# Query projection in three float32r passes, rope in one set, output weights' low part on GpSimd

## What is computed

```python
x = x + xattn(layernorm(x), ctx, ctx)          # sigmoid attention over the context, one head
h = layernorm(x)
c_kv = h @ W_kv_down                           # 512 -> 128
k_rope = rotary(c_kv @ W_k_rope);  k = c_kv @ W_k_up;  v = c_kv @ W_v_up
q = h @ W_q;  q_rope = rotary(h @ W_q_rope)    # 16 heads of 32, rope of 32 shared by the heads
scores = (q·k + q_rope·k_rope) / 8, causal, softmax
x = x + (softmax @ v) @ W_o
x = x + ffn(layernorm(x))                      # 8 experts, top 1, relu(g)^2 * u
```

## Time and profile before

| | us |
|---|---|
| median of 3 runs | 578.97 (578.73 to 578.99) |
| profiled execution | 580.1 |
| its span, first to last instruction | 578.3 |
| PE busy | 570.2 |
| DVE busy | 454.7 |
| ACT busy | 399.6 |
| POOL busy | 1.7 |

### The profile page before, as it was taken

One profiled execution on the slowest core, in us unless ns is written; L12 is line 12 of the kernel. 1 busy time (PEld: TensorE's weight loads), 2 busy tenths in 40 slices (PEclk: granted clock), 3 DMA queues, 4 the chain that ended last, 5 costly groups with the idle time before them and its releaser, 6 DMA issues.

```text
span 578.3 us, 7988 instructions
## 1 busy us (share of the span) xinstructions
PE 570.2 (99%) x2986; PEld 477.8 (83%) x2986; DVE 454.7 (79%) x507; ACT 399.6 (69%) x536; POOL 1.7 (0%) x7
## 2 busy tenths in 40 slices
PE   7999999999999999999999999999999999999998
PEld 4788888888888888888888888888888887867887
DVE  5887878787878898889787978887878787888742
ACT  5876766767677877778777777776767665587321
POOL 1000000000000000000000000000000000000000
PEclk8999999999999999999999999999999999999999
DMA  8567777777778877777778878767676745000201
GB/s 322 189 221 233 246 223 250 225 222 237 218 221 252 240 261 239 243 253 255 224 252 251 254 222 256 231 206 225 212 224 213 227 143 212 1 2 2 73 1 37
DMA packets 33238, 115.89 MB, mean 200 GB/s; under 512 B 4080, under 2 KB 4784, under 8 KB 32944
## 3 DMA queue, kind: packets, MB, share of 16 engines
q1 hardware_dynamic: 32768, 115.05, 62.9%
q10 hardware_dynamic: 432, 0.33, 0.2%
HBM read 114.84 MB, written 0.52 MB: 199 GB/s over the span
## 4 chain that ended last, share of the span: by engine, by line
PE 94%; ACT 2%; DVE 2%; DMA 1%; issue 0%; ACTq 0%
PE ps L384 45%; PE ps L328 23%; PE ps L346 12%; PE ps L876 4%; PE ps L908 2%; PE ps L557 2%; PE ps L764 1%; PE ps L491 1%; ACT w L693 1%; PE ps L671 1%; DMA x_s<-in_x 1%; PE ps L700 1%; PE ps L282 0%; PE ps L467 0%; ACT zh L360 0%
## 5 line engine op out<-in xcount | busy, mean ns | idle before, releaser
L384 PE MATMUL ps<-nh,zh 128*128 128x512 f32 x392 | 144.3, 390 | 0.2 <-ACT zh L360 0.2
L384 PE MATMUL ps<-nh,zl 128*128 128x512 f32 x392 | 144.2, 389 | 0.1
L384 PE MATMUL ps<-nl,zh 128*128 128x512 f32 x392 | 144.1, 389 | 0.0
L361 DVE TENSOR_TENSOR zl<-zf,zh 128x1024 fp32r<-128x1024 f32 x49 | 60.1, 1226 | 82.9 <-ACT zh L360 82.9
L247 DVE TENSOR_TENSOR nl<-rawn,nh 128x1024 fp32r<-128x1024 f32 x97 | 115.4, 1220 | 2.2 <-issue 0.8
L233 DVE TENSOR_TENSOR tl<-rawt,th 128x1024 fp32r<-128x1024 f32 x96 | 112.8, 1216 | 0.0
L244 ACT ACTIVATE nh<-rawn 128x1024 fp32r<-128x1024 f32 x97 | 100.7, 1056 | 13.5 <-DMA rawn<-in_ctxn 12.8
L356 ACT ACTIVATE zf<-ps 128x512 f32<-128x512 f32 x98 | 58.4, 597 | 56.9 <-PE ps L346 51.0
L228 ACT ACTIVATE th<-rawt 128x1024 fp32r<-128x1024 f32 x96 | 96.4, 1052 | 0.9 <-DMA rawt<-in_ctxt 0.8
L384 PEld LDWEIGHTS ps<-nh,zh 128*128 128x128 f32 x392 | 73.4, 188 | 15.9 <-ACT zh L360 0.6
L384 PEld LDWEIGHTS ps<-nh,zl 128*128 128x128 f32 x392 | 73.5, 188 | 15.7 <-DVE zl L361 0.5
(11 more groups left out here) (182 smaller groups left out, 605.0 us busy)
## 6 DMA issues: line engine op xcount, KB each, us to landing
rawn<-in_ctxn SPq DMA_DIRECT2D x97, 512.0 KB, 6.5
rawt<-in_ctxt SPq DMA_DIRECT2D x96, 512.0 KB, 5.0
h_s<-in_wg SPq DMA_DIRECT2D x4, 512.0 KB, 6.7
h_s<-in_wu SPq DMA_DIRECT2D x4, 512.0 KB, 6.9
wds<-in_wd SPq DMA_DIRECT2D x4, 512.0 KB, 5.7
raw<-in_ctxt SPq DMA_DIRECT2D x2, 512.0 KB, 8.3
h_s<-in_wvt SPq DMA_DIRECT2D x2, 512.0 KB, 7.9
wq_s<-in_wq SPq DMA_DIRECT2D x1, 1024.0 KB, 5.0
```

The costliest lines, as they stand in the source:

```text
L361: ZL[b] = put("vector", lambda e: e.tensor_tensor(zl[b % 2][:], zf[:], zh[b % 2][:], ALU.subtract), [ZH[b]] + av, "zl")
L384: AV[b] = put("tensor", lambda e, z=z, n=n, i=i, j=j, r=r: e.matmul(bank(4 + r), z[:, j * T + r * P:j * T + r * P + P], n[:, j * D:(j + 1) ...
```

## The change

It gives the query projection the three-pass form: `wq` is split into `wqh` (ACT) and `wql` (DVE, in place of `wq_s`), `hT` into `hqh` and `hql`. It makes the rope of queries and keys of one row half as one set (both products in one bank, three DVE instructions of 32x256, spreads of 32x2048 on DVE alone), reorders the k copies, moves the subtractions for `wol` from DVE to GpSimd and behind query tile 3, and the first two loads of `wd` behind it too, because `wqh` lies where `wds` is.

```diff
+        wql = once("wql", [P, 4, D], F32R)
...
+        wqh = once("wqh", [P, 4, D], F32R)
         wds = [sb(f"wds{i}", [P, 1024]) for i in range(2)]
         wdh = sb("wdh", [P, 8, D], F32R)
+        hqh, hql = several("hq", 2, [P, 4, T], F32R)
...
-        qa = sa("qa", [P, 8, T])
-        ka = sa("ka", [P, 8, T])
+        qk = sa("qk", [P, 16, T])
+        qa, ka = qk[:, 0:8], qk[:, 8:16]
...
-                    DWD = [dma("sync", wds[k][:], wd[:, 2 * k:2 * k + 2, :].rearrange("p a b -> p (a b)"), f"dwd{k}",
-                               [KP[NB - 1]]) for k in range(2)]
...
         def split_o(k):
...
-            return lambda: put("vector", lambda e: e.tensor_tensor(flat(wol[:, n]), flat(wo_s[:, n]), flat(woh[:, n]),
-                                                                   ALU.subtract), [hi], "wol")
+            return lambda wait: put("gpsimd", lambda e: e.tensor_tensor(flat(wol[:, n]), flat(wo_s[:, n]), flat(woh[:, n]),
+                                                                        ALU.subtract), [hi, *wait], "wol")
+        def split_q(k):
+            n = slice(2 * k, 2 * k + 2)
+            WQH.append(put("scalar", lambda e: e.activation(flat(wqh[:, n]), flat(wq_s[:, n]), ACT.Copy), [DWQ2, KP[last]],
+                           "wqh"))
+            return lambda: WQL.append(put("vector", lambda e: e.tensor_tensor(
+                flat(wql[:, n]), flat(wq_s[:, n]), flat(wqh[:, n]), ALU.subtract), [WQH[k]], "wql"))
+        def split_h(r):
+            n = half(r)
+            HQH.append(put("scalar", lambda e: e.activation(hqh[:, :, n], hT[:, :, n], ACT.Copy), HT[r], "hqh"))
+            return lambda: HQL.append(put("vector", lambda e: e.tensor_tensor(
+                hql[:, :, n], hT[:, :, n], hqh[:, :, n], ALU.subtract), [HQH[r]], "hql"))
...
         table(ACT.Sqrt)
+        low_q = [split_q(0)]
         YA = sum_out(0)
...
         XM = [project_v(0, 2, [ZF[last]])]
+        low_q.append(split_q(1))
         low_o = [split_o(k) for k in range(2)]
...
-        low_o[0]()
+        low_q[0]()
...
-        WOL = low_o[1]()
+        low_q[1]()
+        split_h(0)()
         XM.append(project_v(1, 3, []))
...
-            KR[r] = put("tensor", lambda e: e.matmul(bank(b_c)[:, 0:P], kr_s[:], ckv[:, n], start=True, stop=True),
+            KR[r] = put("tensor", lambda e: e.matmul(bank(b_q)[:, P:T], kr_s[:], ckv[:, n], start=True, stop=True),
...
+        def rope(r, bk):
+            n = half(r)
+            for k in range(2):
+                a = bank(bk)[32 * k:32 * k + 32, 0:T].rearrange("p (w n) -> p w n", w=2)
+                c = cs_s[32 * k:32 * k + 32, n].rearrange("p (o n) -> p o n", o=1).to_broadcast([32, 2, P])
+                m = put("vector", lambda e, k=k, a=a, c=c: e.tensor_tensor(rt[:, k, :, n], a, c, ALU.mult), [KR[r]], "rt")
+            return lambda: put("vector", lambda e: e.tensor_tensor(rt[:, 2, :, n], rt[:, 0, :, n], rt[:, 1, :, n], ALU.add),
+                               [m], "rt")
+        def spread(r, u, mark):
+            n = half(r)
+            d = qk[64 * u + 32:64 * u + 64, :, n].rearrange("p (w s) n -> p w s n", w=2)
+            a = rt[:, 2, :, n].rearrange("p w (o n) -> p w o n", o=1).to_broadcast([32, 2, 8, P])
+            ROT.setdefault(r, []).append(put("vector", lambda e: e.tensor_copy(d, a), [mark], "ro"))
...
+        def query(ts, outs, wait):
+            steps = [(wqh, hqh, HQH + WQH), (wql, hqh, WQL), (wqh, hql, HQL)]
+            for i in range(3):
+                w, h, ready = steps[i]
+                for k, t in enumerate(ts):
+                    n = slice(P * t, P * t + P)
+                    for c in range(4):
+                        done = (i, k, c) == (2, len(ts) - 1, 3)
+                        m = put("tensor", lambda e, w=w, h=h, c=c, i=i, k=k, n=n, done=done: e.matmul(
+                            outs[k], w[:, c, n], h[:, c, :], start=(i == 0 and k == 0 and c == 0), stop=done),
+                            [*ready, *wait], "q" if done else None)
+            return m
...
         values_up(0, 6, 1)
+        add = rope(0, 2)
         HT.append([put("vector", lambda e: e.tensor_scalar(hT[:, 0:2, half(1)], chunks(0)[:, 0:2], 2.0, None, ALU.mult),
...
-        k_copies(0, 4, range(2, 4))
-        f = turned(0, 0, 2, QR[0])
-        spread(0, 0, qa, f, 0)
-        spread(0, 0, qa, f, 1)
+        f = add()
+        low_h = split_h(1)
         latents(1, 5, 7, 3, 0, [YB[1]])
         values_up(1, 0, 1)
+        low_h()
+        spread(0, 0, f)
+        spread(0, 1, f)
+        k_copies(0, 4, range(2, 4))
         VE[0] = put("scalar", lambda e: e.activation(v_s[:, 0, :], bank(6), ACT.Copy), [VT[0]], "ve_a")
         table(ACT.Exp)
-        f = KT0 = turned(1, 0, 1, KR[0])
-        spread(1, 0, ka, f, 0)
-        spread(1, 0, ka, f, 1)
-        k_copies(1, 3)
-        query(0, bank(1)[:, 0:T], [KT0, *HT[1], DWQ2])
-        QT = query(1, bank(1)[:, T:2 * T], [])
-        f = turned(0, 1, 7, QR[1])
-        spread(0, 1, qa, f, 0)
-        spread(0, 1, qa, f, 1)
-        f = turned(1, 1, 5, KR[1])
+        k_copies(1, 3, range(2))
+        QT = query([0, 1], [bank(1)[:, 0:T], bank(1)[:, T:2 * T]], [])
+        g = rope(1, 7)()
+        spread(1, 0, g)
         q_copies(0, QT, bank(1).rearrange("p (t n) -> p t n", t=2), lambda i: slice(i // 2, 4, 2))
-        spread(1, 1, ka, f, 0)
-        QT = query(2, bank(2)[:, 0:T], ROT[0, 0])
+        spread(1, 1, g)
+        QT = query([2], [bank(2)[:, 0:T]], [f])
+        k_copies(1, 3, range(2, 4))
         VE[1] = put("scalar", lambda e: e.activation(v_s[:, 1, :], bank(0), ACT.Copy), [VT[1]], "ve_a")
...
-                [*QA[0], *ROT[0, 0], *ROT[1, 0], KA[0], VE[0]]
+                [*QA[0], *ROT[0], KA[0], VE[0]]
...
         q_copies(1, QT, bank(2)[:, 0:T], lambda i: 4 + i // 2)
-        spread(1, 1, ka, f, 1)
-        QT = query(3, bank(1)[:, 0:T], QA[0])
+        QT = query([3], [bank(1)[:, 0:T]], QA[0])
+        for low in low_o:
+            WOL = low([QT])
+        DWD = [dma("sync", wds[k][:], wd[:, 2 * k:2 * k + 2, :].rearrange("p a b -> p (a b)"), f"dwd{k}", [QT])
+               for k in range(2)]
         exps(0)
```

More of the change, by code:

```diff
@@ L170, in program @@
         v_s = sa("v_s", [P, 2, D])
-        qa = sa("qa", [P, 8, T])
-        ka = sa("ka", [P, 8, T])
+        qk = sa("qk", [P, 16, T])
+        qa, ka = qk[:, 0:8], qk[:, 8:16]
         rtx = ExitStack()
-        rt = rtx.enter_context(nc.sbuf_tensor("rt", [32, 6, T], F32))
+        rt = rtx.enter_context(nc.sbuf_tensor("rt", [32, 3, 2, T], F32))
         rtx.close()
@@ L498, in split_o @@
             hi = put("scalar", lambda e: e.activation(flat(woh[:, n]), flat(wo_s[:, n]), ACT.Copy), [DWO], "woh")
-            return lambda: put("vector", lambda e: e.tensor_tensor(flat(wol[:, n]), flat(wo_s[:, n]), flat(woh[:, n]),
-                                                                   ALU.subtract), [hi], "wol")
+            return lambda wait: put("gpsimd", lambda e: e.tensor_tensor(flat(wol[:, n]), flat(wo_s[:, n]), flat(woh[:, n]),
+                                                                        ALU.subtract), [hi, *wait], "wol")
+        WQH, WQL, HQH, HQL = [], [], [], []
+        def split_q(k):
[9 more added lines that the diff above has]
+                hql[:, :, n], hT[:, :, n], hqh[:, :, n], ALU.subtract), [HQH[r]], "hql"))
         def col(r, k, n=1):
@@ L559, in project @@
             return m
-        CKV, QR, KR, KT, VT = ({} for _ in range(5))
+        CKV, KR, KT, VT = ({} for _ in range(4))
         def latents(r, b_c, b_q, b_k, b_v, wait):
@@ L566, in latents @@
             CKV[r] = put("scalar", lambda e: e.activation(ckv[:, n], bank(b_c)[:, 0:P], ACT.Copy), [m], "ckv")
-            QR[r] = project(bank(b_q)[:, 0:P], lambda c: qr_s[:, c, :], n, [X1[r], YT[1][0]], "qr")
-            KR[r] = put("tensor", lambda e: e.matmul(bank(b_c)[:, 0:P], kr_s[:], ckv[:, n], start=True, stop=True),
+            project(bank(b_q)[:, 0:P], lambda c: qr_s[:, c, :], n, [X1[r], YT[1][0]], "qr")
+            KR[r] = put("tensor", lambda e: e.matmul(bank(b_q)[:, P:T], kr_s[:], ckv[:, n], start=True, stop=True),
                         [CKV[r]], "kr")
@@ L613, in q_copies @@
             QA[g] = done
-        def query(t, o, wait):
-            return project(o, lambda c: wq_s[:, c, P * t:P * t + P], slice(0, T), wait, "q")
+        def query(ts, outs, wait):
[10 more added lines that the diff above has]
+            return m
         latents(0, 1, 2, 4, 6, [])
```

## The result

The changed kernel takes 579.94 us (median of 19 runs, 579.76 to 581.15) against 578.94 for the kernel before (19 runs): a ratio of 1.0017 with a 95% interval of 1.0011 to 1.0024. It is a microsecond **slower**, where a gain of 0.7 was forecast.

The account below looks back on a forecast made before the run. PE matmuls bound the stage up to the first scores, ACT sets the pace after 510.97. PE's 0.86 us saving, with 0.15 given back and copies rounding off, nets -0.69: median 578.3, range 577.3 to 581.0.

Parts of the forecast that it names:

- wol on GpSimd: Output weights' low-part subtractions queued on GpSimd after query tile 3, about 511.0; 2.2 us each, needed at 528.07, costing nothing.
- rival 1: GpSimd holds up DVE's small multiplication behind the second unit's maxima; 1.4 us reach the chain, 579.7; chance 0.33.
- The small step: DVE multiplication by a constant after the second unit's maxima, due at 513.61; held until GpSimd ends at 515.4.
- Cover 0.40: Slack of 0.40 us before the third unit's maxima, leaving 1.4 of the 1.8 us lateness on the chain.
- The three passes: Query tiles 0 and 1 on PE as three float32r passes: 2.88 us in place of 3.46; tile 2 1.44, from 1.73.
- the sum of -0.69: Forecast total: first scores start at about 507.83 in place of 508.52, all other parts adding nothing; median 578.3.
- the sign to look for, 8.4 us: If right, first scores come 8.4 us behind the second half's first latent product, 9.2 before.
- The 0.15 given back by DVE ahead of HT: Rope products and the rows' split delay DVE's half of HT; PE starts at about 499.45 instead of 499.30.
- Splitting wq: ACT copies of 1.05 us fit idle time, leaving 0.85 us cover before the first evacuation; DVE subtractions cost nothing.
- Rival 2: Doubled spreads on DVE run at one element a cycle, 2.28 us each, 1.06 more; 581.6; chance 0.07.
- Rival 3: More is won through hidden slack on DVE and ACT's lighter queue: 577.0 to 577.8, middle 577.4; chance 0.13.
- wd loads: Two wd loads moved behind the wait for query 3 on SP; data wanted 17 us later, so no cost.

## Why the prediction was wrong

The sign was wrong, and one step is to blame: **"wol on GpSimd ... Hidden in any case unless it holds up another engine"** was priced at nothing in the forecast, and rival 1, which gives it a price, got a chance of 0.33 against 0.40. It does hold up DVE: the step takes 2.18 us in place of 0.17, and 1.53 us of that reach the chain. Rival 1 said 579.7; 579.94 was measured. Its steps:

- GpSimd's work: 2.2 each assumed, 2.33 measured; from 511.30 (511.0 forecast).
- The small step is late by 1.8: 2.01 measured (2.18 - 0.17).
- Cover 0.40, so 1.4 on the chain: 1.5 measured.
- The sign to look for was given wrongly: "an idle time of DVE ahead of that small step". The step itself gets longer.

The evidence was at hand: the rows showed that this form of operation is faster out of SBUF than out of PSUM at 128x512, 0.55 against 0.68. That the step over two numbers runs in the same form was inferred from its opcode; its 0.17 us can't show a rate.

The Trainium skill (SBUF — State Buffer, "Who interferes with whom") says that a DVE instruction in a two-port mode and one of GpSimd exclude each other for the whole instruction, and that a DVE instruction with two SBUF inputs contends with a GpSimd one that reads SBUF. The traces here agree: 2.18 us for the step, 3.44 for the two-input subtraction, nothing for reads out of PSUM. The Trainium skill (GPSIMD Engine Reference, 3.1) gives 4497 ns for 2048 elements, thus an estimate of 2.25 for 1024; 2.33 was measured. I gave the rule less weight than it had earned, since no row of before had both engines at work.

The rest, point by point:

- **The three passes: right.** 2.88 us for two tiles forecast, 2.89 measured; with the passes undone the gain is gone (578.98). In the medians the sum of -0.69 is nearly what the kernel with the subtraction moved shows: 578.36 against 579.03, -0.67, with an interval from -0.1 to -1.2. That it comes so close is luck in part: the stage itself got 0.58 shorter (8.64 in place of 9.22 us from the first latent product to the scores), and the sign to look for, 8.4 us, was not met; the changed kernel has 8.67.
- **That sum holds two errors that cancel in part.** The 0.15 given back by DVE ahead of HT isn't there: PE starts at 499.35 where it started at 499.30, with a stream already 0.05 late (first evacuation at 482.40, before 482.35). The first rope product started at 497.90, under the end of the normalisation, and both were through at 498.75 (498.89 forecast); the residual sum, too, began as its data came. In exchange the scores start 0.35 us behind the last copy on DVE (507.67 to 508.02), where 0.04 was put down. Half of that, 0.17, goes with the waits which stand behind the one met last; the rest is open.
- **Splitting wq: right, with less cover.** The weights land at 480.80, 0.4 later than put down, and ACT is idle for 0.55 us ahead of the evacuation instead of 0.85.
- **Rival 2: out.** The spreads of 32x2048 take 1.22 on average, as the double rate had it; DVE is idle for 0.52 ahead of the q copies (0.65 forecast).
- **Rival 3: out.** The exponentials start 2.45 us behind the first scores, as forecast; ACT's lighter queue brings nothing, as the third unit's maxima start 7.74 us behind the first scores in the kernel before and in the one with the later subtraction.
- **wd loads: right.** They land in the same stretch in the kernel without GpSimd's work, and nothing waits.

## What to carry to other kernels

Work moved to GpSimd was free here only when DVE meanwhile ran no multiplication by a constant over two or more numbers per partition from SBUF to SBUF, and nothing with two inputs in SBUF; even a step over two numbers waited for what was left of a GpSimd instruction of 2.33 us. Put each GpSimd instruction behind a DVE step of that kind with a gap as long as itself, by a wait on that step, and look for the loss in the duration of short DVE instructions, not in idle times. When an engine waits for several things, let the wait that is met last stand last; here that brought 0.17 us in the trace. Three float32r passes were cheaper than one float32 product, 2.89 us in place of 3.46 for two tiles, with the splits of the operands hidden beside other work.

## What was not expected

- DVE gets its turn between two GpSimd instructions that stand back to back: twice in the kernel with twice the work, each time within 0.05 us of an instruction's end. In the kernel with GpSimd early the two-input subtraction (1.22) fits between the two in the same way: they take 5.82 us in place of 4.66, 1.16 more.
- A step over one number per partition isn't held (0.15 us at 490.32, GpSimd at work until 490.93), one over two numbers is. This was seen once.
- 2.5 us without work on PE (488.5 to 491.0) came with a granted clock of 0.50 from 490.5 on, and a stage of 2.98 us took 4.84. In that execution the wait cost 2.31 us and the slower PE as much again.
- Four waits that are already met, behind the one that holds PE, delayed the scores by 0.17 us.
